# A hybrid state-space and mixture-of-experts layer: other queue orders, and row sums of squares made with ones as the stationary operand in four column groups

## The reference

```python
x = x + attn(layernorm(x))        # attn itself adds its input again
x = x + ffn(layernorm(x))

# attn: a scan over the tokens, 8 heads of 32, state 64
h = rmsnorm(hidden); z, x, B, C, dt = split(h @ w_in_proj)
x = silu(causal_conv4(x));  dt = softplus(dt @ w_dt + b_dt), mean over a head
y = ssd_scan(x, dt, B, C, A_log) + x * D
y = rmsnorm(y * silu(z)) @ w_out_proj        # mean of squares over 256 channels
# ffn: 2 shared experts (mean) and the best 2 of 4 routed ones, each 128 -> 512 -> 128
shared = mean_n(relu(x @ sw1 + sb1) @ sw2 + sb2)
routed = sum_top2(w_e * (relu(x @ rw1 + rb1) @ rw2 + rb2))
```

## Time and profile before

| | |
|---|---|
| median of 3 runs | 631.07 us (629.84 to 632.64) |
| the profiled execution | 627.16 us, of which 625.4 us is the span from first to last instruction |
| PE, DVE, ACT, POOL busy | 568.7, 448.1, 351.4, 179.6 us |
| TensorE clock over the span | 0.981 of full |

### The profile page before, as it was taken

The page is one execution under the profiler, slowest core; times in us unless marked ns, Lnnn a source line. Parts: engine busy times, 40 slices in busy tenths (PEclk is TensorE's granted clock), DMA queues, the critical chain, the costliest instruction groups (busy, mean ns, idle before and its releaser), DMA issues.

```text
span 625.4 us, 11773 instructions
## 1 busy us (share of the span) xinstructions
PE 568.7 (91%) x3976; PEld 445.0 (71%) x3976; DVE 448.1 (72%) x1049; ACT 351.4 (56%) x753; POOL 179.6 (29%) x233
## 2 busy tenths in 40 slices
PE   6798989998989999899998989899998989989995
PEld 5676867786767777677676767677677866768763
DVE  3879757876679866678679866787677766675653
ACT  3684467637664467527575377535676375742341
POOL 2067104421144214430145211532144202252011
PEclk9999889999999999899999999999998999999999
DMA  7531026100550007200350006400161005500120
GB/s 209 150 108 31 1 81 147 52 1 2 138 157 3 1 29 193 75 1 0 98 178 17 0 0 174 119 0 0 45 198 50 0 1 127 135 18 1 49 40 17
DMA packets 36919, 41.40 MB, mean 66 GB/s; under 512 B 3306, under 2 KB 27284, under 8 KB 36884
## 3 DMA queue, kind: packets, MB, share of 16 engines
q1 hardware_dynamic: 36240, 40.78, 23.3%
q10 hardware_dynamic: 644, 0.17, 0.2%
HBM read 37.79 MB, written 3.15 MB: 65 GB/s over the span
## 4 chain that ended last, share of the span: by engine, by line
PE 29%; DVE 20%; issue 18%; ACT 8%; POOL 6%; DMA 6%; SPq 1%; DVEq 0%; POOLq 0%; ACTq 0%
DMA seg<-lc_rows 5%; PE bank L405 4%; DVE act_l L1219 3%; PE bank L613 3%; PE bank L407 3%; PE bank L406 3%; ACT act_h L835 3%; PE bank L516 3%; PE bank L614 2%; PE bank L615 2%; POOL seg L1424 2%; PE bank L562 2%; ACT seg L855 2%; POOL CTe L1410 2%; PE bank L553 2%
## 5 line engine op out<-in xcount | busy, mean ns | idle before, releaser
L1219 DVE SCALAR_TENSOR_TENSOR act_l<-bank,act_h 128x512 fp32r<-128x512 f32 x192 | 132.0, 688 | 112.1 <-ACT act_h L835 110.2
L835 ACT ACTIVATE act_h<-bank 128x512 fp32r<-128x512 f32 x192 | 114.7, 597 | 83.5 <-PE bank L407 79.8
L1433 POOL TENSOR_TENSOR late<-late 128x512 f32<-128x512 f32 x32 | 46.4, 1451 | 251.1 <-DVE late L1227 251.1
L613 PE MATMUL bank<-act_l,w2h 128*128 128x512 f32 x192 | 79.6, 415 | 23.4 <-DVE late L1227 21.7
L405 PE MATMUL bank<-fTl,w1h 128*128 128x512 f32 x192 | 88.6, 462 | 8.9 <-DVE act_l L1219 6.3
L855 ACT ACTIVATE seg<-seg,lneg 128x128 f32<-128x128 f32 x256 | 81.3, 391 | 26.1 <-DMA seg<-lc_rows 26.1
L407 PE MATMUL bank<-fTh,w1h 128*128 128x512 f32 x192 | 76.2, 397 | 0.0
L406 PE MATMUL bank<-fTh,w1l 128*128 128x512 f32 x192 | 76.1, 397 | 0.0
L614 PE MATMUL bank<-act_h,w2l 128*128 128x512 f32 x192 | 75.9, 395 | 0.0
L615 PE MATMUL bank<-act_h,w2h 128*128 128x512 f32 x192 | 75.9, 395 | 0.0
L613 PEld LDWEIGHTS bank<-act_l,w2h 128*128 128x128 f32 x192 | 36.4, 190 | 41.5 <-DVE late L1227 28.6
(11 more groups left out here) (172 smaller groups left out, 1085.0 us busy)
## 6 DMA issues: line engine op xcount, KB each, us to landing
seg<-lc_rows SPq DMA_DIRECT2D x32, 512.0 KB, 4.7
late<-gk_rows SPq DMA_DIRECT2D x8, 1024.0 KB, 8.5
grow<-lc_rows SPq DMA_DIRECT2D x48, 128.0 KB, 5.2
x_in<-L_attn_hidden_dram SPq DMA_DIRECT2D x8, 256.0 KB, 2.9
out_dram<-late SPq DMA_DIRECT2D x8, 256.0 KB, 2.5
late<-L_ffn_sw_dram SPq DMA_DIRECT2D x2, 512.0 KB, 6.1
late<-L_ffn_rw_dram SPq DMA_DIRECT2D x1, 1024.0 KB, 6.3
CT<-L_attn_w_in_proj_dram SPq DMA_DIRECT2D x1, 772.0 KB, 6.9
```

Of the source, the lines that this page charges most:

```text
L613: mm(FOUT[:], w2h[:, g, k, :], act_l[:, r, :], start=begins, stop=False)
L835: nc.scalar.activation(act_h[:, b % RING, :], HID[b % 2][:], ACT.Relu).then_inc(act_h_ready, 1)
L1219: v_.scalar_tensor_tensor(act_l[:, r, :], HID[b % 2][:], 0.0, f(act_h[:, r, :]), ALU.max, ALU.subtract)\
L1433: g.tensor_tensor(acc, acc, term, ALU.add).then_inc(acc_ready, 1)
```

## The change

**Sums of squares.** Before, `sq` (channels by tokens) was the stationary operand and a single column of ones the moving one, eight times, each giving 128 sums in one column. Now 32 columns of ones are stationary and `sq` moves; the four chunks go to four column groups (output partitions 32c to 32c + 31). ACT copies the 128x128 result to `sqT`, and one matmul with `sqT` stationary and four columns of the identity gives the sums as columns. It stands between the second and third chunk of `out_projection`.

**Queue orders.** `lcs` goes from step 7 to step 8, projection 13 ahead of 12. On ACT, `relu` goes ahead of `b_copy`/`xs_copy` in steps 5 and 6, and ahead of the first `decays` in steps 10 and 11. On DVE, `act_low` goes ahead of `norm2_apply`, all four taps of `conv(s, 1)` come in step 1, and `fT_low` and `act_low` go ahead of `dt_clamp`. On SP, chunk 2's `segments` goes ahead of `wbc`. In the opening, projections 10 and 11 go ahead of `x_tokens`. The last sequence alternates between two output banks (`sum_bank`), and its last term is added by DVE (`last_term`).

```diff
+        def sum_bank(s, b):
+            return MAIN[3] if is_seq(s, n_seq - 1) and (b < 8 or b // 4 in (3, 5)) else FOUT
...
# SP, body
+                if s is not None:
+                    sp_eng.wait_ge(mg_ready, nth(s, 8, 2))
+                    sp_eng.wait_ge(xw_ready, nth(s, 6, 2))
+                    segments(s, 2)
                 if prev is not None:
...
                 if s is not None:
-                    for c in (2, 3):
-                        sp_eng.wait_ge(mg_ready, nth(s, 8, 2 * c - 2))
-                        sp_eng.wait_ge(xw_ready, nth(s, 6, 2 * c - 2))
-                        segments(s, c)
+                    sp_eng.wait_ge(mg_ready, nth(s, 8, 4))
+                    sp_eng.wait_ge(xw_ready, nth(s, 6, 4))
+                    segments(s, 3)
...
# PE
-            def sum_squares(s, c):
-                if c == 0 and is_seq(s, n_seq - 1):
+            def square_rows(s):
+                if is_seq(s, n_seq - 1):
                     pe.wait_ge(btok_ready, nth(s, 3, 3))
-                pe.wait_ge(sq_ready, nth(s, 4, c + 1))
                 for b in range(NB):
-                    ins = mm(TR[:, c:c + 1], sq[:, b, at(c)], ones[:, 0:1], start=(b == 0), stop=(b == NB - 1))
-                if c == NCH - 1:
-                    ins.then_inc(ssq_psum, 1)
+                    for c in range(NCH):
+                        if b == 0:
+                            pe.wait_ge(sq_ready, nth(s, 4, c + 1))
+                        ins = mm(TR[32 * c:32 * c + 32, 0:P], ones[:, 0:32], sq[:, b, at(c)], start=(b == 0), stop=(b == NB - 1))
+                ins.then_inc(sqT_psum, 1)
+
+            def sum_squares(s):
+                pe.wait_ge(sqT_ready, nth(s, 1, 1))
+                mm(TR[:, 2 * P:2 * P + NCH], sqT[:], ident[:].rearrange("p (c q) -> p c q", c=NCH)[:, :, 0], start=True, stop=True)\
+                    .then_inc(ssq_psum, 1)
...
# PE, second(): the last sequence waits one expert later
-                if b == 0:
+                if b == 0 and last:
+                    pe.wait_ge(mg_ready, nth(prev, 8, 8))
+                if b == (8 if last else 0):
                     if (v := nth(prev, 4, 0)) is not None:
                         pe.wait_ge(term_ready, v)
-                if b == 8:
+                if b == (12 if last else 8):
                     pe.wait_ge(shared_ready, nth(prev, 1, 1))
-                if b in (12, 16, 20):
-                    pe.wait_ge(term_ready, nth(prev, 4, b // 4 - 2))
+                if b in ((16, 20) if last else (12, 16, 20)):
+                    pe.wait_ge(term_ready, nth(prev, 4, b // 4 - (3 if last else 2)))
...
# PE, scan_part
                     proj(s, 11)
+                if i == 8:
                     lcs(s)
...
# PE, scan_end
-                for c in range(NCH):
-                    sum_squares(s, c)
+                square_rows(s)
                 for c in range(NCH):
                     out_projection(s, c)
+                    if c == 1:
+                        sum_squares(s)
...
# ACT, after relu in body
+                    if s is not None and i in (5, 6):
+                        b_copy(s, i - 3)
+                        xs_copy(s, i - 5)
+                    if s is not None and i in (10, 11):
+                        decays(s, 0, i - 10)
...
# ACT, scan_end
                 squares(s, NCH - 1)
+                act.wait_ge(sqT_psum, nth(s, 1, 1))
+                if (v := nth(s, 1, 0)) is not None:
+                    act.wait_ge(ssq_psum, v)
+                nc.scalar.copy(sqT[:], TR[:, 0:P]).then_inc(sqT_ready, 1)
...
# DVE
+            def last_term(prev):
+                dve.wait_ge(term_ready, nth(prev, 4, 4))
+                v_.tensor_tensor(acc, acc, term, ALU.add).then_inc(acc_ready, 1)
```

More of the change, by code:

```diff
@@ L159, in build @@
         sq = sb("sq", [P, NB, SEQ])
+        sqT = sb("sqT", [P, P])
         msq = sb("msq", [P, NCH])
@@ L251, in build @@
         sq_ready = sem("sq_ready")
+        sqT_psum = sem("sqT_psum")
+        sqT_ready = sem("sqT_ready")
         ssq_psum = sem("ssq_psum")
@@ L288, in made @@
         def made(s, j):
-            return nth(s, 14, ((j + 2) % 4 if is_seq(s, 0) and j < 4 else j) + 1)
+            if is_seq(s, 0):
+                return nth(s, 14, ((j + 2) % 4 if j < 4 else j) + 1)
+            return nth(s, 14, (25 - j if j > 11 else j) + 1)
         def bodies(eng, opening, body):
@@ L612, in second @@
                     pe.wait_ge(w2l_set, NG)
-                mm(FOUT[:], w2h[:, g, k, :], act_l[:, r, :], start=begins, stop=False)
-                mm(FOUT[:], w2l[:, g, k, :], act_h[:, r, :], start=False, stop=False)
-                mm(FOUT[:], w2h[:, g, k, :], act_h[:, r, :], start=False, stop=ends).then_inc(second_done, 1)
+                mm(dst[:], w2h[:, g, k, :], act_l[:, r, :], start=begins, stop=False)
+                mm(dst[:], w2l[:, g, k, :], act_h[:, r, :], start=False, stop=False)
+                mm(dst[:], w2h[:, g, k, :], act_h[:, r, :], start=False, stop=ends).then_inc(second_done, 1)
             def fold_gate():
@@ L666, in scan_part @@
                     proj(s, 11)
+                if i == 8:
                     lcs(s)
-                if i in (8, 9):
-                    proj(s, i + 4)
+                    proj(s, 13)
+                if i == 9:
+                    proj(s, 12)
                 if i >= CHUNKS_FROM:
@@ L740, in opening @@
                 lcs(0)
+                proj(0, 10)
+                proj(0, 11)
                 x_tokens(0, 0)
                 x_tokens(0, 1)
-                proj(0, 10)
-                proj(0, 11)
                 proj(0, 12)
@@ L846, in shared_out @@
                     act.wait_ge(outT_psum, v)
-                nc.scalar.activation(acc, FOUT[:], ACT.Identity, bias=b2sum[:], scale=0.5).then_inc(shared_ready, 1)
+                nc.scalar.activation(acc, sum_bank(prev, 0)[:], ACT.Identity, bias=b2sum[:], scale=0.5).then_inc(shared_ready, 1)
             def decays(s, c, hf):
@@ L882, in scan_part @@
                     b_copy(s, 1)
[L883 to L887, removed]
                 if i == 7:
+                    c_copy(s, 1)
+                if i == 8:
                     chunk_decays(s)
-                if i in (10, 11):
-                    decays(s, 0, i - 10)
+                    c_copy(s, 3)
+                if i == 9:
+                    c_copy(s, 2)
                 if i >= CHUNKS_FROM:
@@ L973, in opening @@
                 chunk_decays(0)
+                b_copy(0, 2)
+                b_copy(0, 3)
                 silu_x(0, 1)
                 nc.scalar.preload_act_table_set("natural_log_exp_and_others")
-                b_copy(0, 2)
-                b_copy(0, 3)
                 for b in (1, 2, 3):
@@ L1256, in body @@
                 for i in range(NBLK):
-                    if prev is not None:
-                        if i == 1:
-                            norm2_apply(prev)
-                        if i == LATE - 1:
-                            fT_low(prev)
+                    if prev is not None and i == LATE - 1:
+                        fT_low(prev)
                     if s is not None:
@@ L1277, in body @@
                         act_low(*new)
+                    if prev is not None and i == 1:
+                        norm2_apply(prev)
                     if s is not None:
-                        if i in (0, 1):
-                            conv(s, 1, (2 * i, 2 * i + 1))
+                        if i == 1:
+                            conv(s, 1, range(TAPS))
                         if i == 2:
@@ L1283, in body @@
                             dt_add(s, 1)
+                        if i == 3:
                             dt_clamp(s)
@@ L1293, in body @@
                         routed_out(older, 3)
+                        if is_seq(older, n_seq - 1):
+                            last_term(older)
                     if prev is not None and i in (15 + LAG, 19 + LAG):
@@ L1438, in body @@
                     rsqrt2(prev)
-                if older is not None:
+                if older is not None and not is_seq(older, n_seq - 1):
                     add_term(older, 3)
```

10 lines of the change are left out of this document (6 added, 4 removed).

## The result

The kernel takes **591.0 us** (median of 4 runs, 588.8 to 591.7) against 630.5 us for the kernel before (median of 4, 627.4 to 632.6). The ratio is 0.937, 95% interval 0.932 to 0.942. 601 us was forecast, with 592 us as the lower end: right in direction, too small by a quarter, and 1 us outside the range. Ratios leave out executions more than 1.5% above the fastest of the same kernel; medians take in all. The profiled execution takes 591.66 us, of which 589.9 us is the span.

A forecast was written before the change was run, and what follows sets the result against it. TensorE, busy 568.7 of 625.4 us, stands waiting on DVE, itself held by a relu and late `seg`. Bodies 22.2, body 1 2.0, sequence change 0.4, clock 4.2, opening 1.5, drain 2.7: 33.0, cut to 30; 601 us, range 592 to 620.

The forecast's parts named there:

- The walk through the body: One body followed in time order, noting how much earlier PE reaches each place: 3.7 us gained at its end.
- `first` of block 0: DVE's front: with its waits shortened, PE starts block 0 at 362.6 instead of 363.35, 0.75 us earlier.
- thin covers: The broadcast, POOL's `CTe` behind `add_term`, and `mg`: 0.5 us taken off in each of six bodies.
- `lcsT`: With `lcs` one step later, `lcsT` and the SP transfers it feeds move by 0.55 us only (bounds 0 and 1.75).
- the opening's 1.5 us: Opening: `x_tokens` waited 1.59 us for `silu_x` while ready projections stood behind it; 1.5 us gained (bounds 0 and 2.4).
- the sum is taken off both alike: The same gain is subtracted from the profiled execution (627.16 us) and from the median, 3.9 us above it.
- the clock's term: Four clock dips of 1.4 us in bodies 1, 3, 5 and 6; three go, gaining 4.2 us.
- The lower end of the range: Forecast's own range 593 to 608 us: down by the 3 us taken off, the fourth dip and the opening's bound.
- The sums of squares: New sums save PE 0.9 us, but `add_residual` then waits for POOL's `rstd`: 0.25 us gained a body.
- The broadcast did not become the wait: Rival: broadcast starts only after `seg` is through, `routed_out` comes 2.1 us late in six bodies: 618 us, chance 0.2.
- the cases of VectorE, ScalarE: Rival: VectorE or ScalarE becomes the bound, a body gains 1.5 instead of 3.2 us: 611 us, chance 0.15.
- the scan's chain: Rival, slower: front gains nothing, `lcsT` 1.8 us late, six bodies lose 1.2 us: 636 us, chance 0.05.

The follow-up runs named there:

- `before_again`: The kernel before run again with no edit, for a second profile: 631.5 us.
- `sp_only`: The kernel before with only the third chunk of `seg` read ahead of the gate's broadcast on SP: 616.0 us.
- `sp_sums`: The kernel before with the third chunk of `seg` ahead of the gate's broadcast and the new sums of squares: 609.4 us.
- `sp_back`: The changed kernel with the third chunk of `seg` read behind the gate's broadcast again: 618.3 us.
- `rstd_old_sums`: The changed kernel with POOL's `rsqrt_y` ahead of its last `add_term`, but the old sums of squares: 594.2 us.
- `old_sums`: The changed kernel with the sums of squares made in the old way: 594.7 us.
- `store_late`: The kernel before with the output store moved behind the four reads of `seg` and `grow` on SP: 622.1 us.

## Why the prediction was wrong

**What held.** The walk through the body held at each place to about half a microsecond (`first` of block 0, for one, came 0.60 us earlier, 0.75 forecast). Its sum, 3.7 us, is what a dip-free body gained (71.01 to 67.41, 3.60). `add_residual` released by POOL, `out_projection` reached after 0.57 us, the second `seg` group without a wait and bodies of 67.4 us at clock 1.00 were all as said. By the Trainium skill (TensorEngine Tiling (Array Packing), Key Properties) a change of tiling mode drains the array; sixteen records in 0.57 us with the next product right behind leave no room for a drain worth pricing here.

**The step that failed: "At the thin covers ... I take off 0.5 us in each of six bodies".** The three covers held. The broadcast landed 2.0 us ahead, `y_product` (370.56) did not wait for `mg`, and POOL's `CTe` cost PE 0.18 us, as before. I had seen that `seg` could be earlier only with `lcsT`, and missed that on SP it stood behind a store that the change brings forward as well. `lcsT` came only 0.2 us earlier in the body (26.10 us from its start against 26.29) where 0.55 was forecast, but from `lcsT` to `decays` it took 6.0 us instead of 7.3. That put `decays` 1.5 us earlier instead of 0.55, and `mg` and the two transfers behind it too. Taken off wrongly: 3.0 us of the 5.5 us by which the profiled execution came out lower (35.5 us gained, 30 forecast). The other 2.5 us: bodies 2, 3 and 7 gained 3.3 us more than their terms (bodies 3 and 7 had waits of 2.82 and 2.23 us before block 12, longer than in the body that was walked; body 2 had not, and its 0.5 us stays open), body 1 and the drain gained 0.5 us more each, and the opening's 1.5 us did not come.

**The second: "the sum is taken off both alike".** The median of before lay 3.9 us above the profiled execution; that of after lies 0.65 us below its own. So 4.5 of the 10 us between 601 and 591 are the base's, and 5.5 the profiled execution's. By `before_again` a slower execution of the kernel before has more dips and longer waits for the third `seg` (up to 0.6 us a body); the change removes those waits and the old sums, while the dips of the opening stay. So the clock's term, "I let three go: 4.2 us", was counted in an execution that happened to have few dips (five in bodies 1 to 6, since body 1 has two, not the four that were counted). It was also put to the waits alone, while `sp_only` and `sp_sums` show that five dips hang on the old sums.

The lower end of the range does not follow from its own terms either: 601 less 3, 1.4 and 0.9 is 596, not 593 or 592.

**The sums of squares** were priced at 0.25 us a body. Their own part is that (0.1 to 0.4), but with the clock the step is worth 3.7 us in the changed kernel and 6.6 on top of the queue order.

**The rivals.** The broadcast did not become the wait, in the full change or alone. No body gained as little as the cases of VectorE, ScalarE or the scan's chain would have it, though each wait over 0.3 us that is left in a middle body ends with VectorE.

**What stays open.** One edit's worth depends on what stands beside it. The queue order is worth 15 us added to before and 27 us taken from after; the likely reason is that the store and the relu bring the demand for the third `seg` forward, so that its lateness shows in full, but no run took these three apart. A dip does not follow every wait: bodies 7 of before (2.23 us) and 6 of `sp_back` (2.37) have none, body 5 of before (1.79) has one. Nor does a run tell what the clock gate counts in the old sums.

## What to carry to other kernels

Walk one body in order of time and write down at each place how much earlier each engine arrives: that sum held. Do not take a flat sum off for covers that might be thin; compute when each transfer lands and what stands ahead of it in its queue, stores too. Take the base from several executions: where the clock dips in some and not in others, count them in each, and see which code stands ahead of each dip, since the gain of removing a wait and that of another form of the sums are then partly the same thing. And where a faster operation is followed by a small one on another engine, look at what stands in front of that one in its queue: POOL's order hid most of the new sums' own gain (4.9 us).

## What the hardware showed

- Sixteen records of 32 stationary by 128 moving columns in fp32, turning through four column groups, take 0.57 us; sixteen of 128 by one column take 1.71 us.
- TensorE's granted clock fell to 1.2 GHz 1.5 to 2.3 us after the old sums began, with PE counted as busy throughout, in five bodies of `sp_only` (3 to 6 and the first of the drain), three of `rstd_old_sums`, two of `old_sums` and one each of `before_again` and `store_late`: 12 of the 42 starts of bodies 2 to 7 and of the drain in six profiles with the old sums. The eleven profiles with the new sums have no dip in the first 10 us of any such body. In body 1, where TensorE waits about 1.5 us for ScalarE in the midst of the sums, five of these eleven have one at 2 us.
- A transfer of 512 KB issued 0.4 us ahead of one of 1 MB in the same queue landed after 3.5 us, and the large one after 8.8 us, where it had taken 8.5 us when issued first (8.9 in `sp_back`). Issued 1.7 us behind it, the small one took 8.5 us (`sp_back`).
